# Last layer of a four-layer graph network on one core: first head stacks copied during the query products, last query block in two parts around the first scores

## What is computed

```
h = relu(layernorm(x))
q, k, v = split(h @ W)                 # W: 512 x 1536
aw = (q * 64**-0.5)[src] . k[dest]     # per edge and head
alpha = softmax of aw over the edges of each src
out = segment_sum(alpha * v[dest], src)
x = x + out
```

## Time and profile before

| | |
|---|---|
| time, median of 3 | 1279.27 us |
| profiled execution, its time | 1277.57 us |
| its span, first to last instruction | 1275.8 us |
| PE busy | 1146.9 us (90%) |
| DVE busy | 930.5 us (73%) |
| ACT busy | 715.2 us (56%) |
| DMA, mean over the span | 28 GB/s |
| key and query products of the last layer | about 892 to 943 us |
| score loop | about 949 to 1269 us |

### The profile page before, as it was taken

The page is one execution under the profiler, slowest core; times in us unless marked ns, Lnnn a source line. Parts: engine busy times, 40 slices in busy tenths (PEclk is TensorE's granted clock), DMA queues, the critical chain, the costliest instruction groups (busy, mean ns, idle before and its releaser), DMA issues. The chain is left out here.

```text
span 1275.8 us, 17226 instructions
## 1 busy us (share of the span) xinstructions
PE 1146.9 (90%) x6001; PEld 721.6 (57%) x6001; DVE 930.5 (73%) x1686; ACT 715.2 (56%) x902; POOL 65.1 (5%) x115
## 2 busy tenths in 40 slices
PE   3999959997898995979999999969979999999996
PEld 2666634554775553434444544436536777777775
DVE  5999955002755787788989897875337888888885
ACT  1132267303556675337788786845126777777774
POOL 3000042100001200000000000000000000000000
PEclk8999968998999997989999999989989999999999
DMA  4000000003003000203111100000020011110002
GB/s 152 5 1 1 1 1 1 1 1 120 13 1 92 2 1 0 83 23 141 45 43 43 44 22 1 3 1 1 1 50 13 15 26 26 27 26 14 14 1 81
DMA packets 24770, 36.17 MB, mean 28 GB/s; under 512 B 11874, under 2 KB 13204, under 8 KB 24694
## 3 DMA queue, kind: packets, MB, share of 16 engines
q1 hardware_dynamic: 24694, 35.14, 9.1%
HBM read 26.03 MB, written 2.70 MB: 23 GB/s over the span
## 5 line engine op out<-in xcount | busy, mean ns | idle before, releaser
L59 PE MATMUL wide<-arena 125*125 (+9 forms) x2124 | 470.8, 371 | 34.0 <-DVE arena L904 13.3
L59 PEld LDWEIGHTS wide<-arena 125*125 (+5 forms) x2124 | 262.1, 131 | 219.3 <-issue 114.2
L1736 PE MATMUL wide<-arena 125*65 125x512 f32 (+1 forms) x480 | 182.3, 516 | 0.0
L1352 PE MATMUL wide<-ident,arena 125*125 125x125 f32 (+3 forms) x954 | 129.6, 282 | 14.0 <-ACT arena L603 4.7
L734 ACT ACTIVATE arena<-arena,b 125x1250 f32<-125x1250 f32 x80 | 106.7, 1336 | 60.1 <-PE wide L1736 56.0
L1251 DVE TENSOR_TENSOR arena<-wide,arena 125x1250 f32<-125x1250 f32 x80 | 116.7, 1459 | 30.1 <-PE wide L1726 30.0
L1352 PEld LDWEIGHTS wide<-ident,arena 125*125 125x125 f32 (+3 forms) x954 | 114.3, 185 | 24.5 <-issue 10.5
L813 ACT ACTIVATE arena<-wide 125x1000 f16<-125x1000 f32 x80 | 80.8, 1010 | 80.8 <-PE wide L1352 80.8
L1736 PEld LDWEIGHTS wide<-arena 125*65 125x65 f32 x480 | 63.4, 138 | 101.7 <-issue 95.3
L1313 DVE SCALAR_TENSOR_TENSOR arena<-wide,arena 125x1000 f16<-125x1000 f32 x80 | 95.9, 1198 | 33.9 <-ACT arena L813 33.9
L828 ACT ACTIVATE arena<-arena,neg_max,unit 125x1250 f32<-125x1250 f32 x80 | 114.3, 1429 | 10.7 <-DVE neg_max L1340 10.7
(11 more groups left out here) (250 smaller groups left out, 1236.5 us busy)
## 6 DMA issues: line engine op xcount, KB each, us to landing
arena<-rows_kept SPq DMA_DIRECT2D x16, 625.0 KB, 5.9
arena<-arena SPq DMA_DIRECT2D x40, 156.2 KB, 2.9
arena<-in_L_gnn_W SPq DMA_DIRECT2D x3, 1024.0 KB, 7.7
x_nm<-in_x SPq DMA_DIRECT2D x2, 1250.0 KB
out<-x_nm SPq DMA_DIRECT2D x1, 2187.5 KB
arena<-in_L_gnn_W_l SPq DMA_DIRECT2D x1, 1024.0 KB, 5.4
arena<-in_L_gnn_W_r SPq DMA_DIRECT2D x1, 1024.0 KB, 7.9
arena<-in_L_gnn_Wk SPq DMA_DIRECT2D x1, 1024.0 KB, 5.3
```

Of the source, the lines that this page charges most:

```text
L59: mm = pe.matmul(ps[0:rows, lo:hi], lhsT, rhs[:, lo:hi], start=start, stop=stop, skip_group_check=True)
L1352: return pe.transpose(dst, src, ident[0:k, 0:k])
L1736: m = pe.matmul(psW[1][0:VA, lo:hi], v_gat[0:ROWS, t, h, :], ring[n % RINGS][0:ROWS, lo:hi], start=(t == 0), stop=(t == TILES - 1))
```

## The change

SP waits for four finished blocks (the keys) where it waited for eight; its next wait, `proj3_out` of 5, is as it was. The last query block (n = 7) is issued in two parts of 18 matmuls. PE then waits for `proj3_out` of 7 in place of 8, issues `score(0)`, and then the second part; the wait for `proj3_out` of 8 moves to PE's step 2, before the first `turn_tile`, which writes to the same PSUM tile as block 7. ACT takes the upper part of block 7 after exponential 0, and DVE the rest after the bias of step 1.

```diff
@@ sync
-            sp.wait_ge(S["proj3_full"], 2 * KD)
+            sp.wait_ge(S["proj3_full"], KD)
@@ scalar
-                for n in range(2 * KD):
+                def projected_up(n):
+
                     act.wait_ge(S["proj3_full"], n + 1)
                     act.activation((k_hi, q_hi)[n // KD][:, n % KD, :], psW[n % 2][:, 0:N], ACT.Copy, scale=SCALED).then_inc(S["proj3_1"], 1)
+
+                for n in range(2 * KD - 1):
+                    projected_up(n)
...
+                    if n == 0:
+                        projected_up(2 * KD - 1)
@@ vector
-                for n in range(2 * KD):
+                def projected_low(n):
+
                     hi, lo = ((k_hi, k_lo), (q_hi, q_lo))[n // KD]
                     dve.wait_ge(S["proj3_1"], n + 1)
                     stt(lo[:, n % KD, :], psW[n % 2][:, 0:N], SCALED, hi[:, n % KD, :], ALU.mult, ALU.subtract).then_inc(S["proj3_out"], 1)
+
+                for n in range(2 * KD - 1):
+                    projected_low(n)
                     for t in ((2 * n, 2 * n + 1) if n < HEAD_HALF else ()):
                         scaled_logs(t).then_inc(S["log_set"], 1)
...
+                    if n == 1:
+                        projected_low(2 * KD - 1)
@@ tensor
+                def project_half(n, ks):
+
+                    hi, lo = (w16_k, w16_q)[n // KD]
+                    for k in ks:
+                        for i, (w_part, h_part) in enumerate(((hi, hT_hi), (hi, hT_lo), (lo, hT_hi))):
+                            m = wide_matmul(pe, psW[n % 2], 128, w_part[:, k, 128 * (n % KD):128 * (n % KD) + 128], h_part[:, k, :],
+                                            k == 0 and i == 0, k == KD - 1 and i == 2)
+                    if k == KD - 1:
+                        m.then_inc(S["proj3_full"], 1)
+
                 for n in range(2 * KD):
                     pe.wait_ge(*((S["proj3_out"], n - 1) if n >= 2 else (S["v3_out"], TILES - 1 + n)))
                     if n % KD == 0:
                         pe.wait_ge(S["w16_lo"], 4 + n // KD * 2)
-                    hi, lo = (w16_k, w16_q)[n // KD]
-                    for k in range(KD):
...
-                    m.then_inc(S["proj3_full"], 1)
+                    project_half(n, range(KD) if n < 2 * KD - 1 else range(KD // 2))
...
-                pe.wait_ge(S["proj3_out"], 2 * KD)
+                pe.wait_ge(S["proj3_out"], 2 * KD - 1)
                 pe.wait_ge(S["v3_out"], TILES)
                 pe.wait_ge(S["acc_read"], H)
                 score(0)
+                project_half(2 * KD - 1, range(KD // 2, KD))
                 for n in range(H * TILES + 5):
+                    if n == 2:
+                        pe.wait_ge(S["proj3_out"], 2 * KD)
```

More of the change, by code:

```diff
@@ L1787, in _ @@
                         pe.wait_ge(S["w16_lo"], 4 + n // KD * 2)
-                    hi, lo = (w16_k, w16_q)[n // KD]
-                    for k in range(KD):
-                        for i, (w_part, h_part) in enumerate(((hi, hT_hi), (hi, hT_lo), (lo, hT_hi))):
-                            m = wide_matmul(pe, psW[n % 2], 128, w_part[:, k, 128 * (n % KD):128 * (n % KD) + 128], h_part[:, k, :],
-                                            k == 0 and i == 0, k == KD - 1 and i == 2)
-                    m.then_inc(S["proj3_full"], 1)
+                    project_half(n, range(KD) if n < 2 * KD - 1 else range(KD // 2))
                 def score(n):
```

## The result

The changed kernel takes 1266.13 us (median of four runs, 1264.78 to 1267.6), the kernel before 1279.22 us in the same comparison: a ratio of 0.9898, 95% interval 0.9881 to 0.9915. A second comparison gave 1265.70 us against 1277.64, ratio 0.9900 (0.9876 to 0.9924). The profiled execution took 1264.78 us (span 1263.1), 12.79 less than the profiled one of before. Three executions, one each of three_third, whole_block and before_filled, took 2344.58, 4894.86 and 4062.30 us, and are left out of all times, ratios and entries.

What follows compares the result with a forecast made beforehand. The loop is bound by PE; its entry by a hole waiting for copies and a slow clock. Hole 6.09, clock 4.8 and filled pause 1.7, less moved wait 0.6, give 12.0: 1279.27 to 1267.3 us, range 1265.9 to 1270.6.

Steps and rivals of the forecast that it cites:

- What bounded the entry: Start of the score loop: a 6.09 us hole in PE waiting for copies, then a slow start at 1.2 GHz.
- the 4.8 of the sum: Three scores and the first eight transposes at the lower clock: 4.8 us to be regained at the whole clock.
- The copies: SP's ten copies start at 926.74, head 0's land about 932.7, 7.3 us before needed; no cost on other engines.
- PE's order: score(0) inside block 7 without a stop, ending at 941.18; reading 0 at 941.34, second half of block 7 behind.
- The moved wait before the transposes: PE waits for DVE's part of block 7 before the first ten transposes; costs PE about 0.6 us.
- The sum at the whole clock: Gain up to the second ten transposes: 6.09 + 4.8 + 1.7 - 0.6 = 12.0 us, clock at 1.00 throughout.
- The clock in the fill: Open point: PE's clock in the loop's first steps, 945.59 to 949.1, taken as staying at 1.00.
- the row at 824: Kernel before, 824 to 826: PE works 0.26 of 2 us and the clock stays 1.00; taken as nearer neighbour.
- the row at 164 to 168: Kernel before: 2.11 us of PE work in 4, mostly transposes, and the clock ends by falling to 0.5.
- the first rival: Clock falls in the fill at 946 to 950, costing 2.5 us (low end 1.1): 1269.8 us; chance 0.23.
- The two rivals of other sign: Late copies at the first scores, 1279 to 1284 us, chance 0.04; clock staying low, 1282.4 us, chance 0.02.
- The low clock that stays: Clock falls in the fill and stays low while PE is saturated; 1282.4 us with two periods' work; chance 0.02.

Runs made afterwards that it cites:

- three_third: Second profile of the changed kernel with block 7's second half itself parted, its last quarter after the second scores; 2344.58 us, left out.
- whole_block: Changed kernel, but PE issues block 7 whole before the first scores; 1269.36 us, ratio 0.9915 to the kernel before.
- before_filled: Kernel before plus 42 unread matmuls in PE's hole and behind the first two scores; 1274.11 us, ratio 0.9965 to the kernel before.
- idle_filled: Changed kernel plus nine unread matmuls in PE's pauses, after scores 1 and 2; 1265.95 us, ratio 0.9901 to the kernel before.
- copies_at_6: Changed kernel, but SP starts the first copies one block later (proj3_out of 6); 1266.87 us, one run.
- copies_at_7: Changed kernel, but SP starts the first copies two blocks later (proj3_out of 7); 1274.31 us, ratio 0.9960 to the kernel before.
- low_after_0: Changed kernel, but DVE takes its part of block 7 one step earlier, after the bias of step 0; 1268.50 us, one run.
- three_parts: Changed kernel, but block 7's second half is parted again, its last quarter after the second scores; 1264.85 us, ratio 0.9896 to the kernel before.

## Why the prediction was right, and where it was off

It was right in direction, in size (12.0 us forecast, 13.1 and 11.9 in the two comparisons) and in range (1265.9 to 1270.6, measured 1266.13). By its steps, all counted from ACT's copy of block 6:

- **What bounded the entry**: right. The hole is gone, and before_filled confirms that the hole also owned the low clock, with 4.2 us for the 4.8 of the sum. The missing 0.6 is three times the 0.2 that a score costs more when PE starts it after a wait. The change puts the first two scores right behind other matmuls, so by my estimate it gains 0.4 of it, and not the third part.
- **The copies**: issues forecast 10.0 us ahead, measured 9.99; cover forecast 7.3 us. One block (6.4 us) less did no harm, and two blocks less stopped PE by 5.7 us. The cost on other engines was put at nothing, and no row shows one: blocks 5 and 6 still follow each other in 6.39 us, and ACT and DVE take 1.21 and 1.46 us for them.
- **PE's order**: reading 0 forecast at +4.53, measured +4.53. The moved wait before the transposes: DVE's part of block 7 forecast at +10.7, measured +10.69. But the wait cost PE 0.19 us and not 0.6, because the scores ahead of it take 1.42 us and not 1.21.
- **The sum at the whole clock**: 12.0 held, in part because two errors nearly cancel. Redone it is 6.09 + 4.2 + 0.4 + 1.7 - 0.2 = 12.2. idle_filled shows 27.83 - 15.87 = 11.96, with the 0.2 that its added matmuls cost.
- **The clock in the fill**: wrong. The sum had it at 1.00, and it fell in all four profiles whose PE order and waits are the change's (three of the change, one of copies_at_6). I chose between the row at 824 and the row at 164 to 168 by the shortness of the hole, and that is no measure: the pause at 824 is 1.80 us, longer than the 1.71 of the fill, and the clock stayed at 1.00 there in all thirteen profiles (shown at whole_block). What tells the two places apart stays open. It was the mechanism of the first rival, which had 0.23, but at 0.6 to 0.8 us in place of 2.5, below even its low end of 1.1: the low stretch is 3 to 4 us and not 5.35, and only its transposes lie on the path. With it the entry gains 11.4 us and not 12.0.
- **The median**: that the forecast's 12.0 comes so near to 13.1 and 11.9 is partly luck: what the entry lacks, the rest of the kernel gave. The single times spread because the last layer's products do not start at the same moment: ACT's copy of block 6 stands at 934.27 to 938.34 us in thirteen profiles, of ten kernels that have the same instructions up to there but for the copies. The granted clock differs among them in the stretches from about 150 to 600 us. I did not experiment on that part; that the clock there is the cause of the spread is argued, not shown. It means that 13.1 us are not all the change's: by the entry its worth is 11.4.
- **The two rivals of other sign**: copies_at_7 priced the second. With the copies late by 5.7 us the kernel is at 0.9960, still faster than before. My 1279 to 1284 us were for copies landing 9 us late, which was not run; I would now expect less, since in copies_at_7 the clock was back during the half block behind the first scores. The low clock that stays was not seen, but my reason against it, that the clock rises with some us of unbroken work, is weaker than I wrote: in low_after_0 it stayed low through 9 us of it.

The Trainium skill, TensorE: Matmul & The Clock Gate, section "A second HAM failure mode: psum-queue depth-cycling", says that short pauses of PE between groups of matmuls can send its clock down. This case's traces agree that they can: a pause of 1.70 us in whole_block and 1.71 us in the change were each followed by 0.5. The 1.80 us at 824 were not.

## What to carry to other kernels

Where a pipelined loop starts behind a long phase of matmuls, look at the first steps alone: there the pipeline has no other work to cover its waits, and each of PE's pauses can cost a second time through the clock. Keep back part of the phase before and put it into these pauses, and start the loop's copies early enough to land before PE needs them (earlier still gained nothing here, copies_at_6). To price such a fall of the clock, fill the pauses with matmuls that nobody reads: it separates the clock from the wait, if you check that the added matmuls delay nothing.

## What the runs showed of the hardware

- One pause of 1.70 us behind 50 us of unbroken matmuls was followed by the lower clock (whole_block), while one of 1.37 us was not (three_parts, one profile). Nor was one of 1.80 us at 824, in any of thirteen profiles. The length of a pause alone does not tell.
- The clock came back 5.35 us after unbroken work began in the kernel before, and in low_after_0 not before 9 us of it were over.
- Matmuls whose result is not read hold the clock: 42 of them brought the kernel before from 27.83 to 23.60 us in its entry.
- Ten copies beside running matmuls took 2.4/3.3/3.6 us from issue to landing (the change), against 2.4/3.3/3.5 beside a PE idle for most of it (before), and left the matmuls as they were: a block took 6.39 us.
- A score of six matmuls takes 1.39 to 1.42 us when PE starts it after a wait (before_filled), and adds 1.21 us behind other matmuls.
